# A fused attention chain on one core: the three column sums of a narrow step are gathered behind its last values product

## The chip, the cores and the metric

The kernel runs on one core of a Trainium2 chip. The metric is the device time of one execution in microseconds; the time given for the kernel before is the median of three runs.

## The reference, cut to what matters

Eight samples of 256 channels by 32x32 positions (1,024 tokens) go through four attention layers:

- layer 0: group norm, q, k, v, 8 heads of 32 channels, softmax attention, output projection, residual;
- layer 1: group norm, a position term, a spatial gate (three small convolutions), 8 heads of 32 channels, beside it two heads of 128 channels, then two dense layers, an output projection, group norm, residual;
- layer 2: group norm, 8 heads of 32 channels, output projection, residual on the normed input;
- layer 3: group norm, one head of 256 channels, output projection, residual.

Every attention is `softmax(q k^T * scale) v` over 1,024 keys. What matters here is that a softmax needs, for each query, the sum of its 1,024 exponentials, by which the weighted values are divided.

## The kernel before, in words

**Attentions.** The work is a chain of attentions, of kinds "0", "1", "2" (narrow: heads of 32 channels, four heads worked on together), "m" and "3" (wide: heads of 128 or 256 channels). In turn n the order is 0, 2, 1, 3, m, where 2 and 3 belong to the sample of the turn before. Beside each attention runs a `Between`: projections, group norms and convolutions that make the inputs of a later attention, for another sample. There are 24 narrow attentions of four steps each: 96 narrow steps.

**Units.** A narrow step s covers four heads and 512 queries. It has eight items (128 keys each) of four units (one head each): 32 units. Unit u of an attention is step u // 32. TensorE (PE) in one unit writes one bank of scores (`score`, L528); ScalarE (ACT) takes its exponential into `probs` (L826), a ring of three items; GpSimd (POOL) adds the exponentials of items 0 to 5 into `probs_added`, two heads at a time, in ten additions a step (`score`, L1107); four units after an item's first score and two more, PE multiplies the item's four `probs` with the values (`values_narrow`, L562: four column-tiled products into one bank, "av"). The values of item i of step s come in unit 32s + 4i + 6, so those of the last item, 7, come in unit 34 counted from the step's start, that is in the third unit of the next step.

**Sums.** The sums of a step are three groups of four column-tiled products with `ones` into one bank, "sums" (`sums_narrow`, L577): part 0 of the `probs` of item 6, part 1 of item 7, part 2 of `probs_added`, which waits for the ten additions (`p_added`). In the kernel before, part 0 stands behind the values of item 7 in unit 34, part 1 in unit 36, part 2 in unit 38 ahead of the values of item 0 of the next step. The semaphore `full` of the bank rises with part 2. POOL's first addition of the next step (unit 37, that is its unit 5) waits for it (`until_free`, L1099), because it overwrites `probs_added`.

**After the sums.** VectorE (DVE) turns the sums (L965, a transpose out of the bank, unit 39), takes the reciprocal (L969, unit 40), turns it back (L973, unit 41) and multiplies the av bank with it (L988, unit 43). PE's own program gives the sums bank back for reuse in unit 39 and the av bank in unit 43. These offsets are the tuple in `after_step` (L324), under the names SUMMED, TURNED, INVERTED, BACK, NORMED. For wide attentions the tuple is another one.

**Maxima.** The row maxima of the next step's scores are found ahead of it: every four units PE writes four banks at once (`quad`, L626, four row-tiled products of `high_parts`), and DVE reduces one of them in each of the next four units, that of the quad's own unit first (`maximum`, L931, L943). At the end of a step quads come in units 34, 38, 42 and 46, counted as above. Depending on the step the quads are the attention's own or those of the `Between`.

**Banks.** There are eight banks. `take` (L507) hands out the one that has been free longest and makes PE wait until its reader is done; av, sums, the four maxima banks and the products of a `Between` are held until `give`. PE, ACT, DVE, POOL and SyncE (SP) all walk the same list `PLAN` in order; nothing overtakes. In one unit PE does: the score, the rest of the attention that ended (`behind`, up to 13 units beyond its last), the rest of its own, then the `Between`. The rest of an ended attention passes through the same function `rest` (L646) with u = 128 and more, so a fourth step's sums fall into the first units of the following attention, narrow or wide.

**SP** issues the row of maxima (unit 25 of a step), stack copies, weight loads and the output store; the store hangs on the NORMED place of kind "3" alone.

Of the kernel before, what the change touches and what calls it, by code (L numbers as in the profile page):

```python
# [290 lines left out]
def quads_at(att, u):  # L291

    if not att.wide:
        for s in range(1, att.steps):
            n, r = divmod(u - first_quad(s), 4)
            if r == 0 and 0 <= n < QUADS and (s > 1 or n >= EARLY_QUADS):
                return s, n
    return None


def maxima_at(att, u):

    out = []
    if u < att.units:
        for s in range(1, att.steps):
            first = 2 * (u - att.per * (s - 1)) if att.wide else u - first_quad(s)
            for p in range(first, first + (2 if att.wide else 1)):
                if 0 <= p < att.maxima and not (s == 1 and not att.wide and p < GROUP * EARLY_QUADS):
                    out.append((s, p))
    return out  # L310


def columns_at(att, u):

    for s in range(1, att.steps):
        if u == (att.per * (s - 1) + 5 if att.wide else att.per * s - 7):
            return s
    return None
# [3 lines left out]
SUMMED, TURNED, INVERTED, BACK, NORMED = 0, 1, 2, 3, 4  # L322


def after_step(att, u, what):

    off = ((13, 14, 14, 15, 16) if att.wide else (38, 39, 40, 41, 43))[what]
    s, r = divmod(u - off, att.per)
    return s if r == 0 and 0 <= s < att.steps else None


def items_at(att, u):

    if att.wide:
        return [(s, kt) for s in range(att.steps) for kt in range(8) if u == att.per * s + max(4, kt + 3)]
    return [(s, i) for s in range(att.steps) for i in range(8) if u == att.per * s + 4 * i + 6]
# [21 lines left out]
def build_program(nc, x, pos, resident, stream, fold, out):  # L358
    ctx = ExitStack()
    with ctx:  # L360
# [123 lines left out]
        def filling(key):  # L484
            return full[tiles[key][0]]
# [14 lines left out]
        def _(pe):  # L500
# [6 lines left out]
            def take(key, hold=False, says_full=True):  # L507

                bank = min((i for i in range(BANKS) if i not in held.values()), key=lambda i: (given[i], i))
                tiles[key] = bank, uses[bank], fulls[bank]  # L510
                if uses[bank]:
                    pe.wait_ge(read[bank], uses[bank])
                uses[bank] += 1
                fulls[bank] += says_full
                count["turn"] += 1
                given[bank] = count["turn"]
                if hold:
                    held[key] = bank
                return PS[bank]

            def give(key):
                count["turn"] += 1
                given[held.pop(key)] = count["turn"]
# [29 lines left out]
            def sums(bank, probs, start, stop):  # L553
                for j in range(GROUP):
                    ins = mm(bank[D * j:D * j + D, :], ONES[:, 0:D], probs[:, j, :], start, stop,
                             tile_position=(0, D * j))
                return ins

            def narrow_probs(att, s, i):
                return PR[:, (att.item0 + 8 * s + i) % P_RING, :, :]  # L560

            def values_narrow(att, s, i):  # L562
                until_read(pe, ("score", att.index, 32 * s + 4 * i + 3))
                key = ("av", att.index, s)
                if i == 0:
                    take(key, True)
                bank, probs = PS[tiles[key][0]], narrow_probs(att, s, i)
                for j in range(GROUP):
                    h = GROUP * att.head(s) + j
                    ins = mm(bank[D * j:D * j + D, :], VT[:, att.index % 2, i, D * h:D * h + D], probs[:, j, :],  # L570
                             i == 0, i == 7, tile_position=(0, D * j))
                if i < ADDED:
                    ins.then_inc(p_used, 1)
                if i == 7:
                    ins.then_inc(filling(key), 1)

            def sums_narrow(att, s, part):  # L577
                key = ("sums", att.index, s)
                if part < 2:
                    if part == 0:  # L580
                        take(key, True)
                    sums(PS[tiles[key][0]], narrow_probs(att, s, ADDED + part), part == 0, False).then_inc(p_used, 1)
                else:
                    pe.wait_ge(p_added, att.adds0 + att.adds * (s + 1))
                    sums(PS[tiles[key][0]], ADD, False, True).then_inc(filling(key), 1)

            def values_wide(att, s, kt):
                until_read(pe, ("score", att.index, 8 * s + kt))
                keys = [("av", att.index, s), ("av2", att.index, s)][:att.ctiles]
                probs = PR[:, (att.item0 + 2 * s + kt // 4) % P_RING, kt % 4, :]  # L590
                for d, key in enumerate(keys):

                    if kt == 0:
                        take(key, True, d + 1 < att.ctiles)
                    col = (att.head(s) + d) * P
                    ins = mm(PS[tiles[key][0]][:, :], VT[:, att.index % 2, kt, col:col + P], probs, kt == 0, kt == 7)
                    if kt == 7 and d + 1 < att.ctiles:
                        ins.then_inc(filling(key), 1)
                if kt % 4 == 3:
                    ins.then_inc(p_used, 1)  # L600

            def sums_wide(att, s):
                key = ("sums", att.index, s)
                bank = take(key, True)
                pe.wait_ge(p_added, att.adds0 + att.adds * (s + 1))
                mm(bank[:, :], ONES[:, :], ADD[:, 0, :], True, True).then_inc(filling(key), 1)

            def maximum(att, s, p):
                key = ("max", att.index, s, p)
                if not att.wide:  # L610

                    give(key)
                    return
                bank = take(key)
                if s == 0 and p == 0:
                    until_read(pe, ("q", att.index, (1, 1)))
                    until_read(pe, ("k", att.index, (1, 1)))
                q, k = (wide_part(att.kind, o, "hi") for o in "qk")
                qt, kh = divmod(p, NH)
                q0 = s % NH * HALF + qt * P  # L620
                for ct in range(att.ctiles):
                    g = att.head(s) + ct
                    ins = mm(bank[:, :], q[:, g, q0:q0 + P], k[:, g, half(kh)], ct == 0, ct == att.ctiles - 1)
                ins.then_inc(filling(key), 1)
# [21 lines left out]
            def rest(att, u):  # L646
                if att.wide:
                    for s, p in maxima_at(att, u):
                        maximum(att, s, p)
                s = after_step(att, u, SUMMED)  # L650
                if s is not None and att.wide:
                    sums_wide(att, s)
                elif s is not None:
                    sums_narrow(att, s, 2)
                for s, i in items_at(att, u):
                    if att.wide:
                        values_wide(att, s, i)
                    else:
                        values_narrow(att, s, i)
                if not att.wide and u >= 34 and u % 32 in (2, 4) and u < att.units + 5:  # L660
                    sums_narrow(att, u // 32 - 1, (u % 32 - 2) // 2)
                four = quads_at(att, u)
                if four is not None:
                    quad(att, *four)
                if not att.wide:
                    for s, p in maxima_at(att, u):
                        maximum(att, s, p)
                s = columns_at(att, u)
                if s is not None:
                    columns(att, s)  # L670

                s = after_step(att, u, TURNED)
                if s is not None:
                    give(("sums", att.index, s))
                s = after_step(att, u, NORMED)
                if s is not None:
                    for name in ("av", "av2")[:att.ctiles]:
                        give((name, att.index, s))
# [46 lines left out]
            for event, it, i in PLAN:  # L725
# [27 lines left out]
                elif event == "sa1":  # L753
                    nh, part = i
# [4 lines left out]
                elif event == "sa2":  # L759
                    nh, part = i  # L760
# [39 lines left out]
                elif event == "v":  # L800
                    four, part = i
# [576 lines left out]
```

## Time and profile before

| | |
|---|---|
| median of 3 runs | 5533.32 us (5531.68 to 5542.09) |
| profiled execution | 5545.02 us, its span 5543.2 us |
| PE, DVE, ACT, POOL busy | 91%, 51%, 50%, 58% of the span |
| mean granted PE clock | 0.933 |
| DMA | 221.20 MB, mean 40 GB/s |

The profiled execution's span leaves 1.8 us around it. An engine's busy share is of the time in which it worked on at least one instruction. "Idle" time in a row of groups is the time in which the engine had nothing to do just before instructions of that group, and the name behind the arrow is what ended it. In a timeline, rows give the start, the length of the merged piece, the engine and its instructions, and in brackets how long the engine stood idle ahead of it and for whom. One column-tiled group of four products shows as eight matmul records (x8), a quad as four (x4), one score as one.

### The profile page before, as it was taken

To read this page: it belongs to the slowest core of one execution; us is meant where nothing else is said; L and a number is where in the kernel's file an instruction comes from. 1 tells how busy PE (TensorE), PEld (TensorE's weight loads), DVE (VectorE), ACT (ScalarE), POOL (GpSimd) and SP (SyncE) were. 2 spreads that over 40 slices of the span, in tenths; PEclk is the share of its full clock that TensorE was granted. 3 is DMA by queue.
4 is the path that set the end of the run, shared out by engine and by line. 5 is a ranking of instruction groups with operands and counts; after the bars stand their busy time and mean duration, and the time that the engine had idled before them with its cause. 6 is when DMAs were issued, how large, how long until landed. Compare 5 with 4: busy or idle time off the path is not lost.

```text
span 5543.2 us, 63206 instructions
## 1 busy us (share of the span) xinstructions
PE 5032.5 (91%) x22016; PEld 2259.8 (41%) x22016; DVE 2851.5 (51%) x5110; ACT 2752.0 (50%) x4738; POOL 3232.3 (58%) x1777
## 2 busy tenths in 40 slices
PE   7788989999899998999999999999999999899887
PEld 3235333543335433354334543345333453334534
DVE  5345656256553565535655366544566346563362
ACT  3353665345663456524565255652556525555252
POOL 4474667546674476735767357664576636666363
PEclk8899889999899998999989999999899999899999
DMA  2112111022110211102210112101122012120020
GB/s 83 29 29 58 45 45 37 20 58 53 38 30 27 63 48 31 33 21 63 54 40 19 36 49 54 46 12 40 45 54 51 8 44 55 40 52 7 17 49 12
DMA packets 103609, 221.20 MB, mean 40 GB/s; under 512 B 31105, under 2 KB 33409, under 8 KB 103169
## 3 DMA queue, kind: packets, MB, share of 16 engines
q1 hardware_dynamic: 103296, 217.16, 15.1%
q8 instruction: 181, 2.97, 0.2%
q14 instruction: 132, 1.07, 0.1%
HBM read 56.47 MB, written 8.39 MB: 12 GB/s over the span
## 4 chain that ended last, share of the span: by engine, by line
PE 63%; DVE 9%; issue 9%; ACT 9%; POOL 8%; SPq 1%; DMA 1%; POOLq 0%; ACTq 0%; DVEq 0%
PE bank L502 63%; DVE max_cols L943 6%; POOL probs_added L1133 4%; ACT probs L836 3%; POOL probs_added L1120 3%; ACT L836 1%; ACT act L846 1%; DVE dev_squared L1054 1%; DVE stats L1040 1%; ACT act L855 1%; DVE sums_turned L965 1%; SPq L1220 0%; ACT L877 0%; SPq L1209 0%; DVE sums_turned L973 0%
## 5 line engine op out<-in xcount | busy, mean ns | idle before, releaser
L943 DVE TENSOR_REDUCE max_cols<-bank 128x1 f32<-128x512 f32 x3456 | 2183.8, 681 | 1822.3 <-PE bank L502 1818.5
L836 ACT ACTIVATE probs<-bank 128x512 f32<-128x512 f32 x3456 | 1921.2, 599 | 2267.2 <-PE bank L502 2131.4
L1133 POOL TENSOR_TENSOR probs_added<-probs_added,probs 128x1024 f32<-128x1024 f32 x768 | 1801.2, 2369 | 196.4 <-ACT probs L836 195.8
L502 PE MATMUL bank<-q_stack,k_stack 97*128 97x512 f32 (+1 forms) x3584 | 1669.6, 523 | 129.5 <-DVE max_cols L943 66.2
L502 PE MATMUL bank<-probs,v_tokens 128*32 128x512 f32 (+1 forms) x7168 | 1400.0, 649 | 44.1 <-ACT probs L836 44.1
L502 PEld LDWEIGHTS bank<-q_stack,k_stack 97*128 97x128 f32 (+1 forms) x3584 | 666.4, 197 | 891.5 <-issue 461.3
L502 PE MATMUL bank<-act,weight_stream 128*128 128x512 f32 x1792 | 952.8, 632 | 34.2 <-issue 8.3
L1133 POOL TENSOR_TENSOR probs_added<-probs 128x1024 f32<-128x1024 f32 x192 | 452.6, 2369 | 708.8 <-PE bank L502 682.1
L1120 POOL TENSOR_TENSOR probs_added<-probs 128x512 f32<-128x512 f32 x48 | 60.9, 1269 | 883.8 <-PE bank L502 851.9
L502 PE MATMUL bank<-high_parts 32*128 32x512 f32 x3072 | 409.6, 521 | 144.0 <-ACT probs L836 73.6
L502 PEld LDWEIGHTS bank<-probs,v_tokens 128*32 128x32 f32 (+1 forms) x7168 | 329.8, 123 | 515.2 <-issue 362.1
L502 PEld LDWEIGHTS bank<-high_parts 32*128 32x128 f32 x3072 | 160.3, 191 | 830.2 <-issue 752.2
L502 PEld LDWEIGHTS bank<-act,weight_stream 128*128 128x128 f32 x1792 | 327.8, 196 | 344.2 <-issue 278.2
L1120 POOL TENSOR_TENSOR probs_added<-probs_added,probs 128x512 f32<-128x512 f32 x288 | 373.0, 1295 | 57.5 <-ACT probs L836 32.0
L502 PE MATMUL bank<-k_stack 128*128 128x512 f32 x512 | 273.7, 573 | 53.0 <-ACT probs L836 36.2
L1172 POOL TENSOR_TENSOR low_parts<-full_parts,high_parts 128x512 fp32r<-128x512 f32 x192 | 243.9, 1274 | 100.0 <-ACT full_parts L909 100.0
L502 PE MATMUL bank<-weight_stream,act 128*128 128x256 f32 x1024 | 268.4, 391 | 0.0
L965 DVE STREAM_TRANSPOSE sums_turned<-bank 128x512 f32<-128x512 f32 x144 | 101.8, 707 | 321.1 <-PE bank L502 321.0
L502 PE MATMUL bank<-probs,ones 128*32 128x512 f32 x1536 | 225.1, 662 | 0.0
L502 PEld LDWEIGHTS bank<-weight_stream,act 128*128 128x128 f32 x1024 | 189.3, 192 | 71.1 <-issue 48.6
L955 DVE CAST neg_max_t<-bank 16x128 fp32r<-16x128 f32 (+1 forms) x144 | 39.7, 275 | 337.2 <-PE bank L644 337.2
L846 ACT ACTIVATE act<-act,gn_shift,gn_scale 128x512 f32<-128x512 f32 x192 | 148.3, 805 | 126.5 <-DVE gn_shift L1069 126.5
(82 smaller groups left out, 3479.5 us busy)
## 6 DMA issues: line engine op xcount, KB each, us to landing
k_stack<-high_parts SPq DMA_DIRECT2D x384, 128.0 KB, 2.4
q_stack<-high_parts SPq DMA_DIRECT2D x768, 64.0 KB, 2.0
weight_stream<-stream_dram SPq DMA_DIRECT2D x32, 768.0 KB, 4.4
k_stack<-low_parts SPq DMA_DIRECT2D x192, 128.0 KB, 2.4
q_stack<-low_parts SPq DMA_DIRECT2D x384, 64.0 KB, 2.0
act<-x_dram SPq DMA_DIRECT2D x8, 1024.0 KB, 6.5
act<-pos_dram SPq DMA_DIRECT2D x8, 1024.0 KB, 6.0
weight_stream<-stream_dram SPq DMA_DIRECT2D x16, 512.0 KB, 3.7
```

The costliest lines, as they stand in the source:

```text
L502: return nc.tensor.matmul(dst, lhsT, rhs, start=start, stop=stop, **kw)
L836: act.activation(PR[:, m % P_RING, j, :], bank[:, :], ACT.Exp, scale=att.scale).then_inc(reading(key), 1)
L846: act.activation(act_buf(it.turn, dst)[:, t, half(nh)], act_buf(it.turn, src)[:, t, half(nh)], ACT.Identity, scale=GA[:, t:t + 1], bias=GS ...
L855: ins = act.activation(padded_image(it.turn)[D * j:D * j + D, 1 + rows * i:1 + rows * (i + 1), 2 - j:2 - j + SIDE], bank[D * j:D * j + D, ...
L943: dve.tensor_reduce(cols[:, kh, j, qt:qt + 1], bank[:, :], AX.X, ALU.max).then_inc(reading(key), 1)
L955: dve.tensor_copy(NT_[0:att.cols, :], bank[0:att.cols, 0:P]).then_inc(reading(key), 1)
L965: dve.transpose(RT[:, :], bank[:, :]).then_inc(reading(key), 1)
L1040: mark("stats", dve.bn_stats(ST[:, t, nh, :], act_buf(it.turn, src)[:, t, half(nh)]))
L1054: dve.tensor_tensor(SQ[:, :], DV[:, :], DV[:, :], ALU.mult).then_inc(gn_dev, 1)
L1120: pool.tensor_tensor(ADD[:, 0, :], one, two, ALU.add).then_inc(p_added, 1)
L1133: pool.tensor_tensor(ADD[:, js, :], one, two, ALU.add).then_inc(p_added, 1)
L1172: pool.tensor_tensor(low, whole, high.bitcast(F32), ALU.subtract).then_inc(lo_ready, 1)
```

## The change

The offsets of the three groups of sums and of what follows from them become one place: all three groups stand in unit 34, right behind the values of item 7, and are followed by the turn in 35, the reciprocal in 36, the turn back in 37 and the normalization in 38 (before: 39, 40, 41, 43). The bank of sums is given back in unit 35 (before: 39), the av bank in unit 38 (before: 43). Nothing else of the kernel changes; no instruction is added or removed, and the wide attentions keep their offsets.

```diff
 def after_step(att, u, what):
 
-    off = ((13, 14, 14, 15, 16) if att.wide else (38, 39, 40, 41, 43))[what]
+    off = ((13, 14, 14, 15, 16) if att.wide else (34, 35, 36, 37, 38))[what]
     s, r = divmod(u - off, att.per)
     return s if r == 0 and 0 <= s < att.steps else None
 
@@ -650,15 +650,16 @@
                 s = after_step(att, u, SUMMED)
                 if s is not None and att.wide:
                     sums_wide(att, s)
-                elif s is not None:
-                    sums_narrow(att, s, 2)
                 for s, i in items_at(att, u):
                     if att.wide:
                         values_wide(att, s, i)
                     else:
                         values_narrow(att, s, i)
-                if not att.wide and u >= 34 and u % 32 in (2, 4) and u < att.units + 5:
-                    sums_narrow(att, u // 32 - 1, (u % 32 - 2) // 2)
+                s = after_step(att, u, SUMMED)
+                if s is not None and not att.wide:
+
+                    for part in range(3):
+                        sums_narrow(att, s, part)
                 four = quads_at(att, u)
                 if four is not None:
                     quad(att, *four)
```

## Rows read from the trace of the kernel before

**Rows 1.** The page's first part: busy time, share of the span, instructions.
```profile
PE 5032.5 (91%) x22016; PEld 2259.8 (41%) x22016; DVE 2851.5 (51%) x5110; ACT 2752.0 (50%) x4738; POOL 3232.3 (58%) x1777
```

**Rows 2.** Groups by form: busy us, mean ns | idle before them, who ended it.
```profile
L502 PE MATMUL bank<-q_stack,k_stack 97*128 97x512 f32 x3072 | 1466.7, 544 | 129.5 <-DVE max_cols L943 66.2 <-ACT probs L836 34.4 <-DVE group_mean L1055 18.5
...
L502 PE MATMUL bank<-high_parts 32*128 32x512 f32 x3072 | 409.6, 521 | 144.0 <-ACT probs L836 73.6 <-DVE max_cols L943 55.4 <-ACT full_parts L909 12.7
```

**Rows 3.** Timeline of PE through one step's end, from the last values product.
```profile
4040.73 1.06 PE L502 MATMUL bank<-probs,v_tokens 128*32 128x512 f32 x8
4041.61 1.04 PE L502 MATMUL bank<-probs,ones 128*32 128x512 f32 x8
4042.58 0.51 PE L502 MATMUL bank<-high_parts 32*128 32x512 f32 x4
...
4043.87 0.49 PE L502 MATMUL bank<-q_stack,k_stack 97*128 97x512 f32 x1 [0.35 <-DVE max_cols L943]
4044.29 1.06 PE L502 MATMUL bank<-probs,ones 128*32 128x512 f32 x8
4045.29 0.73 PE L502 MATMUL bank<-q_stack,k_stack 97*128 97x512 f32 x2
4045.95 1.07 PE L502 MATMUL bank<-probs_added,ones 128*32 128x512 f32 x8
4046.83 1.04 PE L502 MATMUL bank<-probs,v_tokens 128*32 128x512 f32 x8
4047.80 0.51 PE L502 MATMUL bank<-high_parts 32*128 32x512 f32 x4
...
4049.09 1.12 PE L502 MATMUL bank<-q_stack,k_stack 97*128 97x512 f32 x3 [0.34 <-DVE max_cols L943]
4050.14 1.06 PE L502 MATMUL bank<-probs,v_tokens 128*32 128x512 f32 x8
4051.19 0.51 PE L502 MATMUL bank<-high_parts 32*128 32x512 f32 x4
4052.18 1.10 PE L502 MATMUL bank<-q_stack,k_stack 97*128 97x512 f32 x3 [0.48 <-DVE max_cols L943]
```

**Rows 4.** Timeline of DVE through the same step's end.
```profile
4043.12 2.48 DVE L943 TENSOR_REDUCE max_cols<-bank 128x1 f32<-128x512 f32 x4 [2.65 <-PE bank L502]
4048.34 0.69 DVE L943 TENSOR_REDUCE max_cols<-bank 128x1 f32<-128x512 f32 x1 [2.74 <-PE bank L502]
4048.95 0.71 DVE L965 STREAM_TRANSPOSE sums_turned<-bank 128x512 f32<-128x512 f32 x1
4049.58 0.65 DVE L943 TENSOR_REDUCE max_cols<-bank 128x1 f32<-128x512 f32 x1
...
4052.64 0.67 DVE L988 TENSOR_TENSOR act<-bank,sums_turned 128x512 f32<-128x512 f32 x1
```

**Rows 5.** Timeline of PE: the quad of unit 34 in a step of kind "2".
```profile
2082.73 0.51 PE L502 MATMUL bank<-high_parts 32*128 32x512 f32 x4 [0.96 <-ACT probs L836]
```

**Rows 6.** Timeline of POOL, then PE, at a step's end in the first turn.
```profile
320.64 16.38 POOL L1133 TENSOR_TENSOR probs_added<-probs_added,probs 128x1024 f32<-128x1024 f32 x7
342.33 4.71 POOL L1133 TENSOR_TENSOR probs_added<-probs 128x1024 f32<-128x1024 f32 x2 [5.31 <-PE bank L502]
338.33 0.51 PE L502 MATMUL bank<-high_parts 32*128 32x512 f32 x4 [1.39 <-ACT probs L836]
```

**Rows 7.** Timeline of POOL, then PE, where the additions end latest against the sums.
```profile
3001.54 7.03 POOL L1133 TENSOR_TENSOR probs_added<-probs_added,probs 128x1024 f32<-128x1024 f32 x3
3007.00 1.04 PE L502 MATMUL bank<-probs,ones 128*32 128x512 f32 x8
```

**Rows 8.** Timeline of POOL where a wide attention follows a narrow one.
```profile
1041.19 1.27 POOL L1120 TENSOR_TENSOR probs_added<-probs 128x512 f32<-128x512 f32 x1 [29.29 <-PE bank L502]
```

**Rows 9.** Windows: length, PE, PEld, DVE, ACT, POOL busy (instructions), granted clock, DMA.
```profile
4088.10:4091.50 3.40, 2.32 (x15) 0.70 (x7) 3.40 (x8) 1.63 (x5) 3.40 (x2) 1.00 0.01 5
4091.70:4095.10 3.40, 3.40 (x11) 0.90 (x11) 1.61 (x3) 1.38 (x3) 3.40 (x3) 0.50 0.00 0
```

## Prediction

> **What bounds the kernel now.** I read the page first, to see which engine is full: PE is busy for 5032.5 us of 5543.2, 91%, and no other engine passes 58% [rows 1]. So a change in the order of the work can win only what PE stands idle (about 510 us), what it loses at half its clock, and small seams between its groups. Next I read the groups by form, to see before which of PE's work the idle time lies: 129.5 us before scores and 144.0 us before quads, ended mostly by DVE's maxima (66.2 and 55.4 us) and ACT's exponentials (34.4 and 73.6 us) [rows 2]. Both are waits for a bank that its reader has not let go. Then I read timelines around step ends, where the change is. In the step shown PE waits for DVE three times in 9 us: 0.35, 0.34 and 0.48 us [rows 3]. DVE meanwhile idles 2.65 us ahead of the first quad's maxima and 2.74 us ahead of the second's, and then is full without a break from 4048.34 to beyond 4052.64, because the two turns, the reciprocal and the multiplication stand in that stretch beside the maxima [rows 4].
>
> **The change, part by part.** Nothing is added or taken away; PE's two later groups of sums, DVE's four operations and two releases of banks move. SP issues nothing at the moved places, so no DMA moves and SP's queue is passed by nothing. POOL's program keeps its order too; only what it waits for comes earlier.
>
> Seams (term A). A column-tiled group followed by another takes 0.88 us start to start (4040.73 to 4041.61, 4045.95 to 4046.83); followed by anything else 0.97 to 1.00 us (4041.61 to 4042.58, 4044.29 to 4045.29, 4046.83 to 4047.80) [rows 3]. Before, five groups cost 0.88 + 0.97 + 1.00 + 0.88 + 0.97 = 4.70 us; after, four in a row and the values of item 0 alone cost 3 x 0.88 + 0.97 + 1.00 = 4.61. That is 0.1 us x 96 steps = 10 us. The row shows the next group's first product starting before the last of the group before has ended (4041.61 against 4040.73 + 1.06), and I take it. The Trainium skill, "TensorE: Matmul & The Clock Gate", section "What overlaps and what doesn't", says that weight loads overlap running products only where the row groups differ; these tiles share theirs, so by that rule a merged group would hide nothing, term A would be 0, and the sum below 10 us smaller.
>
> Banks and DVE (term B). I replay the step of [rows 3] with the new order, at its own durations: a maximum 0.62 us (2.48 / 4, [rows 4]), the turn 0.63 (4048.95 to 4049.58), and from 4048.34 to 4052.64 five maxima (units 38 to 42) plus turn, reciprocal and turn back take 4.30, so these three cost 4.30 - 5 x 0.62 = 1.20 together, and the multiplication about 0.6. PE: the three groups start at 4041.61, 42.49 and 43.37, the quad at 4044.34, which is 1.76 late. DVE starts 0.54 later (as 4042.58 and 4043.12 show) and runs maximum, turn, maximum, reciprocal, maximum, turn back, maximum, multiplication, so these end about at 45.5, 46.15, 46.8, 46.95, 47.6, 48.2, 48.8 and 49.4. PE's score of unit 36 still waits for the first maximum; then scores (0.35 each), values and the quad of unit 38 at 4047.65, where it was 4047.80: the 1.76 us are made up at once, since no sums stand between. The bank of sums is back four units earlier, so one bank more turns from here on. The score of unit 39 waits for the fourth maximum (to 48.9), that of unit 42 for a maximum that ends at 50.0, and the quad of unit 42 starts at 4051.35, 0.16 later than before. Behind it DVE has no multiplication left and the av bank is free, so the 0.48 wait goes; the next work stands 0.3 to 0.5 us earlier. I take 0.35 us for such a step end, of it 0.1 the seam: B = 0.25 us. In each of the seven full turns ten ends have quads in units 34 to 46 (four in kind "0", four in "2", two in "1"): 70 x 0.25 = 17 us. Bounds: +0.16 (nothing regained behind unit 42) to -1.2 (all three waits of 0.35, 0.34, 0.48 gone), that is +11 to -84 us.
>
> Covered waits (term C). In steps where ACT works off a normalization at unit 34, the quad waits 0.96 us for an exponential [rows 5]. The two groups put ahead of it are 1.76 us of work that needs nothing of that exponential, so the wait goes whole. I count ten such ends (kinds "2" and "1", first step) at 0.9 us: 9 us. Bounds 0 to 14.
>
> POOL (term D). In the first turn's kinds "0" and "1" and in the last "2" POOL is the slow one: a step's additions run back to back, end at 337.02 (320.64 + 16.38), and the next step's first one starts at 342.33, after 5.31 us idle for the sums of unit 38 [rows 6]. With the sums in unit 34 it waits only for its own exponentials, up to unit 37. From 337.02 six exponentials follow, units 32 to 37. The first three end some 1.6 us later; PE's quad stands at about 338.65, the scores behind it feed the other three until about 341.3. That is 1.0 us earlier, and as the additions are the cycle here, the step gets shorter by it. PE's 1.39 us wait of [rows 6] is filled by the moved groups. Ten such ends: 10 us, bounds 0 to 25 (half of the 5.31 us).
>
> The wait for the additions moves from unit 38 to 34. Behind it on PE stand the quad and all scores, for which ACT and DVE wait. In the tightest place the additions end at 3008.57 and the first sums start at 3007.00 [rows 7]; two groups later is 3008.76. It holds by 0.19 us there and by more elsewhere, because the exponential of unit 32 waits for the same additions. I cost it at 0; where POOL were late, at most the 1.57 us by which its end passes the first sums, in 18 ends: 28 us.
>
> Where wide follows narrow, POOL stands idle 29.29 us for sums that come in wide units [rows 8], and low parts are queued behind it. PE is full there, so I take 0, bounds 0 to -4.
>
> The half clock (term E). PE fell to 1.2 GHz right behind a stretch in which it was busy 2.32 of 3.40 us, and the next 3.40 us are at 0.50 [rows 9]. About fourteen such falls lie behind these step ends, of 3.4 us each, half of which is lost: 24 us in all. Fewer waits should spare some; I take half, 12 us, bounds -35 (longer falls spared) to +24 (as many new ones).
>
> **Sum:** 10 + 17 + 9 + 10 + 12 = 58 us. Against the profiled execution: 5545 - 58 = 5487. Its time is 11.7 us above the median of the runs, so the forecast for the median is 5475.
>
> **Rivals.** (1) DVE becomes the bound: slower. Up to the quad of unit 34 DVE idles 1.76 us longer than now, and from there to the quad of unit 46 it has 0.54 + 11 x 0.62 + 1.8 = 9.2 us of work, PE 3 x (0.44 quad + 1.45 scores + 1.0 values) = 8.7. That is nearly a tie: where a `Between` adds work of DVE (projection outputs, statistics) without as much for PE, the late start is not made up. It decides from about 0.5 us more of DVE's work than of PE's. For: the quad of unit 42 comes out 0.16 late even in the replay. Against: most ends have projection products beside them, and PE then has the longer list. Price: 0.6 us in 70 ends, +42, B and E gone, A, C, D staying (-29), and 1.7 us for each of a dozen new falls of the clock, +20: +33, that is 5566. (2) The waits only move: PE waits as long for DVE at unit 39 to 42 as it does now, the exponentials of term C come late again, and seams and half of D stay: about -12, 5521. The page's rule on weight loads would make it -6, 5527. (3) The clock answers strongly: bank waits and the falls behind them go nearly all; 24 + 35 of falls and half of the bound of B (42) on top of A, C and D less overlaps: -110, 5423. (4) The sums wait for POOL after all: +28 against the forecast, 5503. That the change does nothing is excluded by the row of POOL's 5.31 us idle, whose releaser it moves.
>
> **How the numbers follow.** About 0.2%, 11 us, can be told from no change. Forecast 0.56 (5445 to 5510), rival 4 0.08, rival 3 0.11, rival 2 0.13, rival 1 0.12. Faster: 0.56 + 0.08 + 0.11 and a few hundredths of rival 2, 0.77. Same: 0.11. Slower: 0.12. The range takes the forecast, rivals 4 and 2 and most of 3: 5425 to 5533.
>
> **What would show it.** In the profile after: PE's groups `probs,ones` x16 and `probs_added,ones` behind the values in one run of about 3.5 us; POOL's first addition idle for ACT rather than PE, and its total idle for PE down by some hundreds of us, the 29.29 us wait to some 10; the quad of unit 34 without the 0.96 us wait; PE's idle before scores and quads down from 273 us to about 220; DVE's two turns within 4 us of that quad; mean clock up from 0.933 to about 0.937. The forecast is wrong if PE's idle ended by DVE grows (rival 1), if PE waits for `probs_added` in narrow steps (rival 4), or if the clock falls.

## The result and the profile after

Each ratio below sets the runs of a kernel against runs of the kernel before on the same chip, with a 95% interval. The kernels of the experiments ran on three chips, so a ratio of two such ratios can cross from one chip to another.

| | before | after |
|---|---|---|
| median of 5 runs each | 5542.09 us (5531.68 to 5547.81) | 5500.40 us (5494.59 to 5509.12) |
| ratio | 1 | 0.9931 [0.9915, 0.9947] |
| profiled span | 5543.2 us | 5492.8 us |
| mean granted PE clock | 0.933 | 0.933 |

By the ratio the change makes the kernel 0.69% faster, 38 us, where 58 us (1.05%) were forecast. In the profiled executions the span is 50.4 us shorter, and nearly all of that, 47.6 us, is PE's busy time; its idle time, span less busy, is 507.9 us, where it was 510.7 [rows 1]:

```profile
span 5492.8 us, 63206 instructions
...
PE 4984.9 (91%) x22016; PEld 2273.7 (41%) x22016; DVE 2860.7 (52%) x5110; ACT 2745.2 (50%) x4738; POOL 3235.1 (59%) x1777
```

The groups by form answer to [rows 2] (busy us, mean ns | idle before them and who ended it), with POOL's and one of DVE's beside them:

```profile
L502 PE MATMUL bank<-q_stack,k_stack 97*128 97x512 f32 x3072 | 1455.4, 542 | 152.3 <-DVE max_cols L944 52.9 <-ACT probs L837 40.7 <-DVE group_mean L1056 30.9
...
L1134 POOL TENSOR_TENSOR probs_added<-probs 128x1024 f32<-128x1024 f32 x192 | 454.5, 2370 | 665.3 <-ACT probs L837 654.6 <-PE bank L502 9.7
L502 PE MATMUL bank<-high_parts 32*128 32x512 f32 x3072 | 412.9, 525 | 132.2 <-DVE max_cols L944 58.6 <-ACT probs L837 55.3 <-ACT full_parts L910 11.0
...
L1055 DVE TENSOR_TENSOR dev_squared<-deviation 128x2 f32<-128x2 f32 x48 | 86.9, 1811 | 1.7
...
L1121 POOL TENSOR_TENSOR probs_added<-probs 128x512 f32<-128x512 f32 x48 | 61.0, 1270 | 771.9 <-PE bank L502 740.3 <-ACT probs L837 31.5
```

The releasers moved as the change says: POOL's first addition of a narrow step now waits for ACT, not for PE. But PE's idle time before scores and quads did not fall: 284.5 us against 273.5. Waits for DVE's maxima fell by 10 us (121.6 to 111.5), yet a releaser that is no part of the change, `group_mean` of the group norm, rose from 18.5 to 30.9 us.

**The end of [rows 3] after the change.** Timeline of PE:

```profile
4003.17 1.06 PE L502 MATMUL bank<-probs,v_tokens 128*32 128x512 f32 x8
4004.05 1.90 PE L502 MATMUL bank<-probs,ones 128*32 128x512 f32 x16
4005.77 1.04 PE L502 MATMUL bank<-probs_added,ones 128*32 128x512 f32 x8
4006.74 0.51 PE L502 MATMUL bank<-high_parts 32*128 32x512 f32 x4
...
4008.02 0.97 PE L502 MATMUL bank<-q_stack,k_stack 97*128 97x512 f32 x3 [0.35 <-DVE max_cols L944]
4008.91 1.06 PE L502 MATMUL bank<-probs,v_tokens 128*32 128x512 f32 x8
4010.12 0.50 PE L502 MATMUL bank<-high_parts 32*128 32x512 f32 x4
4011.11 1.69 PE L502 MATMUL bank<-q_stack,k_stack 97*128 97x512 f32 x4 [0.48 <-DVE max_cols L944]
...
4013.73 0.50 PE L502 MATMUL bank<-high_parts 32*128 32x512 f32 x4
4014.16 0.97 PE L502 MATMUL bank<-q_stack,k_stack 97*128 97x512 f32 x3
4015.01 1.12 PE L502 MATMUL bank<-act,weight_stream 128*128 128x512 f32 x2
...
4017.30 0.51 PE L502 MATMUL bank<-high_parts 32*128 32x512 f32 x4
```

and of DVE:

```profile
4007.27 0.69 DVE L944 TENSOR_REDUCE max_cols<-bank 128x1 f32<-128x512 f32 x1 [4.38 <-PE bank L502]
4007.88 0.71 DVE L966 STREAM_TRANSPOSE sums_turned<-bank 128x512 f32<-128x512 f32 x1
...
4010.98 0.67 DVE L989 TENSOR_TENSOR act<-bank,sums_turned 128x512 f32<-128x512 f32 x1
```

Counted from the last values, the quads of units 34, 38 and 42 stand at +3.57, +6.95 and +10.56; before at +1.85, +7.07 and +10.46. The 1.72 us by which the first is late are made up within four units, the third is 0.10 late, as the replay said (0.16). The four column-tiled groups take 3.57 us, forecast 3.61. Behind unit 42 three scores go through in 0.85 us (4014.16 to 4015.01) with no wait. The quad of unit 46 comes at +14.13, 0.8 us earlier than before.

**Where the rest went.** I laid the two traces side by side, each step cut at PE's first product of each item's values, and summed the differences. From the values of item 7 (values 7, for short; items are counted from 0) to values 4 of the next step, the change gains 92 us over the 95 ends: 36 us of PE's idle time, 14 us lost at half clock before, and 42 us of time in which PE counts as busy, seams and waits that the idle column does not show. The whole span gained 50. So 42 us came back in other stretches, above all in two:

- kinds "2" and "1", step 0, from values 5 to values 7: 28 us in 14 steps, where the group norm's square stands;
- kind "1", step 2, from values 5 to values 7: 16 us in 7 steps. Small differences of the other sign, 2 us, make up the sum. Between values 4 and values 7 PE idles 33 us more than before, which is why its total idle time has hardly moved. The end behind each of these steps loses too, 10 us in all, and has done so inside the 92: some 25 us at this place.

The first place. Before, timeline of POOL, DVE and PE:

```profile
4100.36 9.35 POOL L1133 TENSOR_TENSOR probs_added<-probs_added,probs 128x1024 f32<-128x1024 f32 x4
...
4107.49 2.24 DVE L1054 TENSOR_TENSOR dev_squared<-deviation 128x2 f32<-128x2 f32 x1
...
4109.85 0.73 PE L502 MATMUL bank<-q_stack,k_stack 97*128 97x512 f32 x2 [1.43 <-DVE group_mean L1055]
```

After, the same place:

```profile
4060.64 9.32 POOL L1134 TENSOR_TENSOR probs_added<-probs_added,probs 128x1024 f32<-128x1024 f32 x4
...
4066.45 3.53 DVE L1055 TENSOR_TENSOR dev_squared<-deviation 128x2 f32<-128x2 f32 x1
...
4070.11 0.73 PE L502 MATMUL bank<-q_stack,k_stack 97*128 97x512 f32 x2 [2.73 <-DVE group_mean L1056]
```

A square of 128x2 elements ends when POOL's run of additions ends: at 4109.73 beside 4109.71 before, at 4069.98 beside 4069.96 after. Counted from the start of that run it begins 7.13 us in before and 5.81 us in after, and ends at the same point, 9.3 us. What the step had gained until there is waited away. It is so throughout: of the 48 squares after the change, 13 meet no POOL instruction and take 160 ns, and each of the other 35 ends within 22 ns of the end of one of POOL's additions. Then the clock falls. Windows of after (columns as in [rows 9]; the clock is the last but two):

```profile
4066.00:4069.90 3.90, 1.38 (x13) 0.38 (x5) 3.87 (x4) 0.76 (x2) 3.90 (x2) 1.00 0.01 2
4071.10:4074.50 3.40, 3.40 (x17) 1.19 (x17) 1.86 (x4) 1.21 (x3) 0.00 (x0) 0.62 0.00 0
```

PE was busy 1.38 of 3.90 us at full clock (2.4 GHz), and in the window that begins 1.2 us later the mean granted clock is 0.62, that is, mostly at the 1.2 GHz level. Over the 48 squares the mean went from 1458 ns to 1811. The Trainium skill, "SBUF — State Buffer", section "SBUF: two separate sides", says that a DVE operation with two SBUF inputs and a GpSimd operation that reads SBUF exclude each other on a shared port pair for a whole instruction; this is called the lock below. The trace agrees in kind; the wait was longer, though: 3.53 us against 2.37 for one addition, so DVE got no turn between two of them. In 21 of the 35 squares it waited past the end of an addition into the next, where before it did so in 4; in 7 it did get in between two additions, after 0.56 us. What decides between the two, no run shows.

The second place: kind "1", step 2, item 7, timeline of after:

```profile
4310.30 7.00 POOL L1134 TENSOR_TENSOR probs_added<-probs_added,probs 128x1024 f32<-128x1024 f32 x3
4312.75 2.06 ACT L837 ACTIVATE probs<-bank 128x512 f32<-128x512 f32 x4 [3.81 <-POOL probs_added L1134]
...
4313.40 0.49 PE L502 MATMUL bank<-q_stack,k_stack 97*128 97x512 f32 x1 [1.58 <-ACT probs L837]
```

and the same additions and exponentials before:

```profile
4353.50 7.03 POOL L1133 TENSOR_TENSOR probs_added<-probs_added,probs 128x1024 f32<-128x1024 f32 x3
4355.96 2.06 ACT L836 ACTIVATE probs<-bank 128x512 f32<-128x512 f32 x4 [1.65 <-POOL probs_added L1133]
```

The ring of `probs` holds three items, and POOL must have read an old one before ACT writes. POOL works through this step almost without a pause in both kernels; the step arrives earlier and waits longer. Counted from PE's values of item 5 (4352.18 before, 4306.70 after), POOL's last run of three additions starts 1.32 us in before and 3.60 us in after. Behind the longer wait the clock falls: of the 10 us that the seven ends behind these steps lose, all is the clock's part.

**An end where DVE is the bound.** Seven ends of kind "0", step 0, have statistics of a group norm on DVE beside them. Timeline of PE after, beginning with the first wait behind the sums:

```profile
3925.44 0.95 PE L502 MATMUL bank<-q_stack,k_stack 97*128 97x512 f32 x3 [0.34 <-DVE max_cols L944]
3926.72 1.06 PE L502 MATMUL bank<-probs,v_tokens 128*32 128x512 f32 x8 [0.33 <-DVE max_cols L944]
3928.02 0.51 PE L502 MATMUL bank<-high_parts 32*128 32x512 f32 x4 [0.24 <-DVE max_cols L944]
3928.91 0.50 PE L502 MATMUL bank<-q_stack,k_stack 97*128 97x512 f32 x1 [0.38 <-DVE max_cols L944]
...
3930.10 1.33 PE L502 MATMUL bank<-q_stack,k_stack 97*128 97x512 f32 x3 [0.58 <-DVE max_cols L944]
```

Five waits, 1.87 us; before it was two in the same stretch, 0.69 us, both in these rows:

```profile
3961.72 0.50 PE L502 MATMUL bank<-q_stack,k_stack 97*128 97x512 f32 x1 [0.34 <-DVE max_cols L943]
...
3966.95 0.38 PE L502 MATMUL bank<-mean_var,weights 128*128 128x2 f32 x2 [0.35 <-DVE max_cols L943]
```

That is rival 1's mechanism at its place, but in seven ends, 1.0 us each by the traces side by side, and not in seventy.

### The profile page after: what moved, and what is told of

Its sections match the earlier page's. It is cut to its first block, busy times and chain, and to the rows that moved or that the text cites. A ratio compares the mean times of both kernels' runs of the same rounds, so it can differ in the third digit from the quotient of the medians.

```text
span 5492.8 us, 63206 instructions
## 1 busy us (share of the span) xinstructions
PE 4984.9 (91%) x22016; PEld 2273.7 (41%) x22016; DVE 2860.7 (52%) x5110; ACT 2745.2 (50%) x4738; POOL 3235.1 (59%) x1777
## 4 chain that ended last, share of the span: by engine, by line
PE 59%; issue 11%; DVE 11%; POOL 10%; ACT 7%; SPq 1%; DMA 1%; POOLq 0%; ACTq 0%; DVEq 0%
PE bank L502 59%; DVE max_cols L944 6%; POOL probs_added L1134 6%; ACT probs L837 3%; POOL probs_added L1121 2%; DVE dev_squared L1055 1%; ACT L837 1%; DVE stats L1041 1%; ACT act L847 1%; POOL k_stack L1173 1%; DVE sums_turned L966 1%; ACT act L856 1%; POOL act L1155 1%; SPq L1221 0%; ACT L878 0%
## 5 line engine op out<-in xcount | busy, mean ns | idle before, releaser
L502 PE MATMUL bank<-act,weight_stream 128*128 128x512 f32 x1792 | 938.7, 624 | 20.7 <-issue 8.3
L502 PE MATMUL bank<-q_stack 128*128 128x512 f32 x512 | 203.9, 455 | 3.6 <-DMA neg_row<-neg_max_t 2.1
```

What stands on the lines that cost most here:

```text
L502: return nc.tensor.matmul(dst, lhsT, rhs, start=start, stop=stop, **kw)
```

## The experiments

First, which part of the change carries the gain. The tuple holds the units of the sums, the turn, the reciprocal, the turn back and the normalization. **All groups in unit 34, DVE's operations and the banks as before:**

```diff
-    off = (... else (34, 35, 36, 37, 38))[what]
+    off = (... else (34, 39, 40, 41, 43))[what]
```

> The three groups stand in unit 34, but the turns, reciprocal, multiplication and both releases of banks stay in 39 to 43. If the grouping alone makes the gain (seams, the covered wait for an exponential, the additions' earlier start), this comes out like the whole change, 0.993 of before (about 5500 us). If the earlier releases and the earlier DVE work carry a good part of it, about half is left: 0.9965 (5522 us). If the late DVE work is what hurts because the bank of sums is now held for five units with nothing gained, it is above 0.998.

Measured: 0.9935 [0.9916, 0.9954].

**Only the normalization and the av bank as before:**

```diff
+    off = (... else (34, 35, 36, 37, 43))[what]
```

> As the change, but the multiplication and the release of the av bank stay in unit 43. Two av banks overlap again in units 38 to 43. If the number of turning banks is what PE waits for, a fourth to a third of the gain goes: 0.995 (5514 us), with more PE idle ended by DVE. If DVE's own load in units 35 to 38 is the limit, moving 0.67 us out of it makes it no slower or a little faster: 0.992 to 0.993.

Measured: 0.9899 [0.9881, 0.9917].

**Before, with the second group of sums moved up too, the third and all the rest left:**

```diff
-    if not att.wide and u >= 34 and u % 32 in (2, 4) and u < att.units + 5:
-        sums_narrow(att, u // 32 - 1, (u % 32 - 2) // 2)
+    if not att.wide and u >= 34 and u % 32 == 2 and u < att.units + 5:
+        sums_narrow(att, u // 32 - 1, 0)
+        sums_narrow(att, u // 32 - 1, 1)
```

> Before, with part 1 of the sums moved from unit 36 to 34 alone; part 2 and all that follows stay in 38 and later. It holds one seam of 0.1 us in 96 steps (10 us), the earlier release of the last probs of the ring, and half of the cover for the quad's wait, but neither POOL's earlier start nor any bank. My theory: 0.9975 of before (5528 us). If the seam is worth nothing, as the Trainium skill's rule on weight loads would have it, only the cover stays: 0.999. If PE's groups standing together is the main thing: 0.995.

Measured: 0.9936 [0.9920, 0.9952].

Read alone, these say that one group moved by two units gives all of the change's gain (35 us, where the expectation had 14), that the rest is worth nothing, and that a late normalization is better. Next, **the change with the lock taken away**: the deviation is written to the PSUM bank as well, and the square takes one input from there, so that it has one SBUF input. It costs one more small DVE operation per norm.

```diff
+    mark("dev", dve.tensor_tensor(bank[:, 4:4 + CT], MV[:, :, 0], bank[:, 0:CT], ALU.subtract))
...
-    dve.tensor_tensor(SQ[:, :], DV[:, :], DV[:, :], ALU.mult).then_inc(gn_dev, 1)
+    dve.tensor_tensor(SQ[:, :], bank[:, 4:4 + CT], DV[:, :], ALU.mult).then_inc(gn_dev, 1)
```

> The change, and the group norm's deviation written a second time, into its PSUM bank, so that its square has one SBUF input and one PSUM input (one small DVE operation more, 48 times). In the profile after, the square of 128x2 takes 1811 ns on the mean and up to 3568, where the shortest is 160; PE waits behind it. If DVE stands locked out by POOL's additions because both inputs lie in SBUF, its mean falls to about 160 ns, 80 us of DVE and 20 to 30 us of the time go: 0.988 of before (5475 us). If it only waits its turn behind something else, nothing changes: 0.993.

Measured: 0.9758 [0.9739, 0.9777], median 5407.06 us. Its groups by form:

```profile
L1056 DVE TENSOR_TENSOR dev_squared<-bank,deviation 128x2 f32<-128x2 f32 x48 | 7.6, 159 | 1.7
...
L502 PE MATMUL bank<-q_stack,k_stack 97*128 97x512 f32 x3072 | 1439.0, 537 | 119.1 <-DVE max_cols L944 50.3 <-ACT probs L837 39.0 <-DVE act L1082 7.4
```

The square's mean falls from 1811 to 159 ns, and `group_mean` is gone from the first three releasers. Just as many squares as before, 35 of 48, meet a POOL instruction; none takes more than 163 ns. The time falls more than three times as far as was expected. In the two traces side by side (5492.8 and 5411.8 us) 60 of the 81 us lie between values 5 and values 7 of the 16 steps with kind "1" or "2", step 0, and 34 of these 60 are time lost at half clock, which the expectation had left out. The control, **the same edit in the kernel before**:

> The kernel before, with the deviation written into its PSUM bank too, as in dev_psum. The mean of the square was 1458 ns before the change and 1811 after. If the lock took back part of what the change gains, this gains less than dev_psum did over the change (0.9758 / 0.9931 = 0.983): 0.988 of before (5475 us), and the change without the lock is then worth 1.2% (dev_psum over this). If the lock cost both kernels the same, this stands at 0.983 (5447 us) and the change stays worth 0.7%.

Measured: 0.9916 [0.9903, 0.9930]. So the lock cost the kernel before 0.84% and the changed one 1.7% (0.9758 / 0.9931 = 0.9826). Without it the change is worth 0.9758 / 0.9916 = 0.984, 1.6%; the intervals of the two, in quadrature, leave 0.0024 on it. The profiled spans, one execution of each, go the same way: 5488.9 to 5411.8, 77.1 us or 1.4%. Side by side, these two traces differ by 79.5 us in the step ends, so on balance nothing comes back elsewhere; the first stretch, a loss of 28 us with the lock, is a gain of 4 without it, while the second place, with the end behind it, still loses 25.

The second stretch was tried on **the change with POOL adding one item less in it** (kind "1", step 2, from the second turn: five items by POOL, the sixth summed by PE behind its values):

```diff
+        self.five = 2 if kind == "1" and turn else -1
...
+def items_added(att, s):
+    return ADDED - (s == att.five)
...
+                        if s == att.five and i == ADDED - 1:
+                            sums_narrow(att, s, -1)
```

> The change, but in step 2 of kind "1" (from the second turn on) POOL adds the exponentials of five items and not of six; PE sums item 5 itself in unit 26, a group of 0.9 us more, seven times (+6 us of PE), 33 us of POOL less. In the profile after, PE waits 1.6 and 1.0 us for exponentials that wait 3.81 us for POOL in that step, and the clock falls behind it: 25 us lost there against the trace of before in seven ends. If POOL bounds that step, that comes back less the 6 us: 0.9965 of the change, 0.990 of before (5486 us). If something else does, it is 6 us slower than the change: 0.994.

Measured: 0.9934 [0.9921, 0.9946]. In the trace that step and the end behind it are 6 us shorter over the seven turns: +5.5 for PE's extra group, then -5.0 from values 6 to values 7, where ACT had waited, and -6.4 in the end behind, all of it time lost at half clock. The bound by POOL there is seen, but about half of what it gives back is paid for on PE, and the total can't be told from the change as made. **Both edits together:**

> dev_psum and five_added in one. The lock and the additions sit in different steps (the first in step 0 of kinds "1" and "2", the second in step 2 of kind "1"), so if both readings hold, the gains add: 0.972 of before (5389 us). If the time that the one gives back is lost at the other, it stands where dev_psum does, 0.976.

Measured: 0.9754 [0.9740, 0.9767]; the same as the square's edit alone.

Then the parts again, without the lock. **All groups in unit 34 only:**

> group_only with the deviation in PSUM: the groups in unit 34, DVE and banks in 39 to 43, no lock. group_only came out equal to the whole change (0.9935 and 0.9931), though its step ends gain 36 us in the traces and those of the change 92. If the lock and POOL hid the difference, it shows here: 0.982 of before, against 0.9758 of dev_psum. If the early DVE work and banks are really worth nothing, it equals dev_psum.

Measured: 0.9845 [0.9831, 0.9858].

**Second group moved up only:**

> two_at_34 with the deviation in PSUM: only part 1 of the sums has moved, to unit 34. Beside before_dev_psum (0.9916) and group_dev (0.9845) it says what the second seam, the cover of both groups and POOL's earlier start are worth. If the seams of 0.1 us carry the grouping, half of group_dev's gain: 0.988. If POOL's earlier start and the third group behind the others carry it, 0.990.

Measured: 0.9874 [0.9851, 0.9897].

**DVE's operations early, but both banks counted as given back in units 39 and 43, as before:**

```diff
-                s = after_step(att, u, TURNED)
+                s = after_step(att, u if att.wide else u - 4, TURNED)
...
-                s = after_step(att, u, NORMED)
+                s = after_step(att, u if att.wide else u - 5, NORMED)
```

> dev_psum, but PE's program takes the two banks back into its round in units 39 and 43 as before, while DVE's turns, reciprocal and multiplication stay early. If what the early tail brings (0.9845 to 0.9758) is banks, this falls back to 0.983. If it is that DVE's four operations stand where DVE is otherwise free, it keeps 0.977. I give the banks two thirds: 0.981.

Measured: 0.9968 [0.9955, 0.9981]. Its timeline of PE through the end of [rows 3], from the quad of unit 34:

```profile
4033.51 0.51 PE L502 MATMUL bank<-high_parts 32*128 32x512 f32 x4
...
4034.80 0.96 PE L502 MATMUL bank<-q_stack,k_stack 97*128 97x512 f32 x3 [0.35 <-DVE max_cols L944]
4036.09 1.06 PE L502 MATMUL bank<-probs,v_tokens 128*32 128x512 f32 x8 [0.33 <-DVE max_cols L944]
4037.98 0.50 PE L502 MATMUL bank<-high_parts 32*128 32x512 f32 x4 [0.83 <-DVE max_cols L944]
...
4039.23 1.11 PE L502 MATMUL bank<-q_stack,k_stack 97*128 97x512 f32 x3 [0.31 <-DVE max_cols L944]
```

The quad of unit 38 comes 4.47 us behind that of unit 34; with the banks back early it is 3.38 (4006.74 to 4010.12, above). PE waits on DVE for a free bank four times in these rows.

**Late normalization without the lock,** and **with five items as well:**

> dev_psum with the multiplication and the av bank in unit 43. av_late came out at 0.9899 where the change had 0.9931. If that was a place for DVE's multiplication better in itself, this is 0.3% under dev_psum: 0.973. If it was where the lock and the clock's falls happened to lie, it is at or above dev_psum, 0.976 to 0.979, since the step ends gain 85 us in its trace and 92 in the change's.

Measured: 0.9757 [0.9735, 0.9778], the same as with the early one.

> av_late_dev with five additions in step 2 of kind "1". Beside av_late_dev it says again what the five additions are worth; both over dev_psum was 0.9754 over 0.9758, nothing that can be told. Expected 0.001 below av_late_dev, 0.972 to 0.977.

Measured: 0.9752 [0.9730, 0.9773].

| step, without the lock | ratio to the step above |
|---|---|
| before | 1 |
| second group in unit 34 | 0.9874 / 0.9916 = 0.9958 |
| third group too | 0.9845 / 0.9874 = 0.9971 |
| DVE's operations early, banks late | 0.9968 / 0.9845 = 1.0125 |
| banks early too: the change | 0.9758 / 0.9968 = 0.9789 |

The first two intervals of this table (about 0.0027 each side) leave their sizes rough. The last two steps are beyond doubt: early operations alone are a loss of 1.2%, early banks a gain of 2.1%, 0.9% together (0.0024 each side; the two profiled executions differ by 28.4 us, 0.5%). In the kernel as changed that 0.9% can't be seen (0.9931 against 0.9935, with intervals of 0.002 each side): the lock hid it. The traces with the lock say the same: with the groups alone in unit 34 the square's mean is 1466 ns, as good as the 1458 of before, and with the whole change it is 1811. Against the groups alone the whole change gains 56 us at the step ends and loses 33 us again in the stretches with squares, 31 of them by the half clock, and 16 in the second place.

The advantage of the late normalization, 0.9899, vanished with the lock as well, and why stays open. It did not come from shorter squares: their mean in that trace is 1865 ns. Against the change as made, the second place with its ends is 27 us shorter there, because the step arrives later and waits less, and the rest is 18 us longer; without the lock the second place is again some 27 us shorter, and yet the total is the same.

## Why the prediction was right, and where not

The sign, and a time inside the range, were right (5500 in 5425 to 5533); the likeliest, 5475, was 25 us too low. The terms were less right than the sum, since errors of both signs met in it: the step ends gained more than was forecast, and much of it came back at two places that were in no term. That the sum came as near as it did is in part luck.

- **Seams (A), 10 us:** held. Four groups in a row stand 0.86 to 0.88 us apart and 0.97 before the quad. The rule of the Trainium skill, "TensorE: Matmul & The Clock Gate", section "What overlaps and what doesn't", that weight loads overlap running products only across row groups, by which this term would be 0, is not borne out for these column-tiled groups.
- **Banks and DVE (B), 17 us:** right in mechanism, too small. The replay was within 0.1 us at three quads, but behind unit 42 it took only the 0.48 us wait of [rows 3] as gone. Before, the three scores behind that wait took 1.19 us start to start (4052.18 to 4053.37), and now 0.85: a wait that the idle column does not show. The end gains 0.8 us, not 0.35. Over all 95 ends the gain, less the clock's part, is 78 us; A to D together had 46.
- **Covered waits (C), 9 us:** gone as said. In kind "2", step 0, the quad of unit 34 follows the three groups with nothing between:

```profile
4078.26 1.04 PE L502 MATMUL bank<-probs_added,ones 128*32 128x512 f32 x8
4079.23 0.50 PE L502 MATMUL bank<-high_parts 32*128 32x512 f32 x4
```

- **POOL (D), 10 us:** the step that failed first. Its first addition behind [rows 6]'s run in the first turn:

```profile
338.53 4.75 POOL L1134 TENSOR_TENSOR probs_added<-probs 128x1024 f32<-128x1024 f32 x2 [5.86 <-ACT probs L837]
```

  The idle time is no shorter than 5.31 us, only its releaser has changed. Ends of the first turn gained 1.4 to 1.5 us in step 1, nothing in step 0, and lost 0.4 to 0.5 in step 2, the clock's part aside; with 2.5 us in step 3 that is 4.5 us of the 10. I had read the releaser as the bound; the exponentials behind it were as late. Over the whole run, POOL's idle time before its additions that PE ended fell from 1534 to 750 us, as said, but that which ACT's exponentials ended rose from 286 to 958. The same holds in [rows 8]: the longest such wait is 25.6 us, where I expected some 10.
- **The clock (E), 12 us:** some 5. The time at half clock went from 745 to 735 us, half of which is lost, and the mean is 0.933 in both. At step ends it cost 14 us less, but in the rest of the steps 10 us of that came back on balance; behind the locked squares alone it was 23.
- **What was in no term:** both places that gave back. I followed the moved instructions to the next quads, and not to the next thing on another engine whose time does not move with them: the end of a run of POOL's additions. With the lock away, the change gives 1.6%, above the 1.05% forecast; that the second place still loses its 25 us shows that only the first is mended.
- **Rivals.** Rival 1's mechanism is real: in kind "0", step 0, it shows in the change as made, 7 us, and with DVE's operations early and the banks late, where PE waits for DVE's maxima too, the kernel is 0.5% slower than the one before with the same square (0.9968 / 0.9916). Its count, 70 ends, was wrong. Rival 4 didn't come: in the groups by form PE idles 0.0 us before its products of `probs_added` in narrow steps, and its weight loads for them waited 2.4 us in all. Rival 2's picture, waits that only move, is what the totals look like (507.9 us idle after 510.7), though for another reason than the one it gave: the waits went at the ends and came back in the middle of other steps. Rival 3's amount of 110 us was not reached.

## What to carry to other kernels

When a stretch gets faster, ask what it arrives at next that keeps its own time: a neighbour's run on another engine gives an early comer nothing but a longer wait. Before judging the parts of a change one by one, look for an operation whose duration is far above its size (1811 ns for 128x2 elements, 160 at best), for it can hide what the parts are worth: here 0.9% looked like nothing. And move the release of a buffer together with the work that frees it: here the early work cost 1.2% as long as its banks came back late.

## What the runs showed of the hardware

- A DVE operation with two SBUF inputs stood up to 3.57 us beside back-to-back POOL additions of 2.37 us; with one input from PSUM it took 159 ns at the same place, beside the same additions.
- Two operations with two SBUF inputs still stand longer than their shortest time, `gn_scale` from `rstd` and `weights`, and one in kind "3" that adds the residual; their tiles' views in the kernel without the square's lock (min/median/max ns):

```profile
L1000 DVE SCALAR_TENSOR_TENSOR act<-av_normed,folded_bias,act x32: 752/933/1849, 1069.6 to 5406.6; 128x512 f32<-128x512 f32 x32
...
L1068 DVE TENSOR_TENSOR gn_scale<-rstd,weights x48: 149/160/2312, 29.6 to 5305.0; 128x2 f32<-128x2 f32 x48
```

  The mean of `gn_scale` is 471 ns, so some 15 us in all over the 48 (48 x 0.31); that of the other is 1206, so again some 15 us (32 x 0.45). What they are worth on the path was not tried. `gn_shift`, which has two SBUF inputs as well and comes right behind `gn_scale`, never took more than 221 ns.
- At full clock column-tiled groups of four products follow each other in 0.86 to 0.88 us, whether their weights are `ones` or `v_tokens`; a quad or a score behind one starts 0.97 to 1.00 us after it.
